# One fourth-layer product for two chunks, and a score tile ahead of the values, in a one-core vision layer

## The reference

```
h = concat(cls_tok, tok(x))
h = h + attention(layernorm(h))        # 16 heads of 16 features, causal
h = h + feed_forward(layernorm(h))

# attention, per head: queries and keys of low rank, RMS norm, q = [qn, W_QR qn], k = [kn, W_KR x]
out = softmax(q k^T / 4 + causal) v W_O^T

# feed forward
gf = sigmoid(gelu(gelu(mean_t(x) w1 + b1) w2 + b2) w3 + b3)          # global net: 256-128-64-1, one number per image
for _ in range(3):
    tf = sigmoid(gelu(gelu(gelu(out w1+b1) w2+b2) w3+b3) w4 + b4)    # coupling net: 256-256-128-64-1, one per token
    coupling = 0.1 + adaptive_range * (0.7 gf + 0.3 tf - 0.5) * 2
    out = out + coupling * twist(out)                                # twist swaps the halves, with signs
```

## Time and profile before

| | |
|---|---|
| median of three runs | 3649.94 us (3648.4 to 3652.1) |
| profiled execution | 3651.66 us, its span 3649.9 us |
| PE busy | 3549.6 us, 97% |
| PEld busy | 2676.6 us, 73% |
| DVE busy | 3088.9 us, 85% |
| ACT busy | 2422.8 us, 66% |
| POOL busy | 1827.4 us, 50% |
| mean granted PE clock | 0.989 of full speed |

### The profile page before, as it was taken

How to read it: one execution, slowest core, us unless ns; L and a number is a source line. 1 busy time by engine, 2 the same in 40 slices (tenths; PEclk the granted TensorE clock), 3 DMA queues, 4 the chain that set the end, 5 groups by cost and what they waited for, 6 DMA issues and landing times.

```text
span 3649.9 us, 88155 instructions
## 1 busy us (share of the span) xinstructions
PE 3549.6 (97%) x30735; PEld 2676.6 (73%) x30990; DVE 3088.9 (85%) x7415; ACT 2422.8 (66%) x5698; POOL 1827.4 (50%) x2967
## 2 busy tenths in 40 slices
PE   7999999999999999999999999987999999999998
PEld 6888888888888888888888888875555555555554
DVE  6888888888888888888888888876989989989987
ACT  4777777777777777777777777774554555554554
POOL 5776677666776667766777667763001001001000
PEclk9999999999999999999999999988999999999999
DMA  3444444444444444444444444433222222212211
GB/s 102 119 120 106 117 115 120 114 111 116 117 120 112 114 113 120 116 111 114 117 120 115 113 117 115 120 88 81 65 65 78 71 58 81 75 55 80 73 45 54
DMA packets 298324, 361.76 MB, mean 99 GB/s; under 512 B 28192, under 2 KB 264992, under 8 KB 297888
## 3 DMA queue, kind: packets, MB, share of 16 engines
q1 hardware_dynamic: 297888, 356.11, 37.2%
HBM read 131.80 MB, written 53.26 MB: 51 GB/s over the span
## 4 chain that ended last, share of the span: by engine, by line
PE 86%; DVE 7%; DMA 2%; issue 2%; SPq 1%; ACT 0%; POOL 0%; DVEq 0%; another core or an unknown queue 0%; POOLq 0%
PE ps L1077 14%; PE ps L1411 11%; PE ps L1165 8%; PE ps L1126 7%; PE ps L1113 7%; PE ps L1420 6%; PE ps L1196 5%; PE ps L1150 5%; PE ps L1215 4%; PE ps L1205 3%; PE ps L1173 3%; PE ps L1435 2%; PE ps L1427 2%; PE ps L1154 2%; PE ps L1198 2%
## 5 line engine op out<-in xcount | busy, mean ns | idle before, releaser
L1077 PE MATMUL ps<-xb,w_tok 128*128 128x196 f32 x3072 | 686.3, 348 | 7.5 <-DMA clsT<-in_clsT 7.3
L1411 PE MATMUL ps<-X,cn_w 128*128 128x394 f32 x1536 | 584.9, 510 | 7.7 <-DVE X L1015 7.7
L886 DVE TENSOR_REDUCE mx<-ps 69x2 f32<-69x396 f32 x1024 | 518.0, 553 | 14.2 <-PE ps L1205 1.3
L592 ACT ACTIVATE p<-ps 128x394 f32<-128x394 f32 x1024 | 454.8, 499 | 74.6 <-PE ps L1126 65.3
L1077 PEld LDWEIGHTS ps<-xb,w_tok 128*128 128x128 f32 x3072 | 491.7, 192 | 8.0 <-DMA clsT<-in_clsT 7.3
L880 DVE TENSOR_REDUCE mx<-ps 128x4 f32<-128x512 f32 x512 | 337.6, 680 | 181.1 <-remote 180.2
L543 POOL TENSOR_SCALAR ve<-mv 128x4 f32<-128x4 f32 x64 | 20.2, 316 | 911.7 <-DVE mv L898 911.7
L1411 PEld LDWEIGHTS ps<-X,cn_w 128*128 128x128 f32 x1536 | 273.6, 189 | 258.0 <-issue 94.9
L537 POOL TENSOR_TENSOR h<-h,att 128x256 f32<-128x256 f32 (+1 forms) x256 | 186.9, 751 | 431.9 <-DVE att L875 431.9
L1126 PE MATMUL ps<-qZ,kT 128*128 128x396 f32 (+1 forms) x2048 | 382.5, 320 | 12.9 <-DMA qZ<-mx_scratch 11.0
L610 ACT ACTIVATE sq<-ps 128x256 f32<-128x256 f32 (+1 forms) x512 | 196.2, 383 | 247.1 <-PE ps L1113 247.1
(11 more groups left out here) (139 smaller groups left out, 8076.5 us busy)
## 6 DMA issues: line engine op xcount, KB each, us to landing
qZ<-qT SPq DMA_DIRECT2D x256, 396.0 KB, 5.2
xb<-in_x SPq DMA_DIRECT2D x128, 588.0 KB, 7.2
kZ<-kT SPq DMA_DIRECT2D x512, 128.0 KB, 2.6
h_scratch<-h SPq DMA_DIRECT2D x128, 128.0 KB
hl<-h_scratch SPq DMA_DIRECT2D x64, 256.0 KB
hk<-h_scratch SPq DMA_DIRECT2D x64, 256.0 KB
out<-hk SPq DMA_DIRECT2D x64, 256.0 KB
h_scratch<-h SPq DMA_DIRECT2D x128, 69.0 KB
```

Of the source, the lines that this page charges most:

```text
L592: s.activation(p0[:, i, 2 * jj:2 * jj + 2, :], ps[:, (b0, b1)[jj], 0:2 * TE].rearrange("p (a b) -> p a b", b=TE)[:, :, 0:T], ACT.Exp).then ...
L886: v.tensor_reduce(mx[:T1, 1, 4 * i + c:4 * i + 4:2], ps[:T1, SBANK[3 * i + 1 + c], 0:2 * TE].rearrange("p (a b) -> p a b", b=TE), AX.X, AL ...
L1077: mm = t_.matmul(ps[:, W[ft], 0:NP], w_tok[:, k, ft * P:ft * P + P], xb[:, par, k, :], start=k == 0, stop=k == KT - 1)
L1411: mm = t_.matmul(ps[:, 2 * c + mt, 0:N2], cn_w1[:, f, mt * P:mt * P + P], X[:, c, state(cyc), f, :], start=f == 0, stop=f == FT - 1)
```

## The change

Four things are changed.

1. Layer 4 is one product of 128 rows. `cn_w4r` is now block diagonal: the weights stand in rows 0 to 63 for columns 0 to 63 and in rows 64 to 127 for columns 64 to 127, and zeros elsewhere. So output partitions 0 to 63 hold the first chunk's result, 64 to 127 the second's, in one bank. As `th` must hold each chunk's result in all 128 partitions, ACT now runs two tanh passes of 64 partitions for each chunk: four passes per turn in place of two.
2. The last product of the global net is padded to 128 rows with zeros (`gc_w3r`, `ga2`).
3. DVE clears and fills these tiles once, ahead of the second stage: six operations in place of two, and one more wait.
4. The first tile of group 2 (`scores_first(m, 2)`, with its waits) stands ahead of the values of image o. Banks 0 and 1 change their roles in several tables, so that this tile's bank is freed by the second reduction (`MAX_OF` 2) instead of the fourth.

```
-        SBANK = (6, 7, 0, 1, 2, 3, 0, 1, 2, 3, 0, 5)
-        MAX_OF = (4, 2, 5, 6, 7)
+        SBANK = (6, 7, 0, 1, 2, 3, 1, 0, 2, 3, 1, 5)
+        MAX_OF = (2, 4, 5, 6, 7)
...
             def tanh(i, cyc, c):
-                act.wait_ge(l4_done[c // 2], (i * CYCLES + cyc) * 2 + c % 2 + 1)
-                s.activation(th[:, c, :], ps[:, 4 * (c // 2) + 3 * (c % 2), 0:N2], ACT.Tanh, bias=cn_b4[:, 1:2],
-                             scale=0.5).then_inc(th_ready[c], 1)
+                G, e = divmod(c, 2)
+                rows = slice(e * F3, e * F3 + F3)
+                act.wait_ge(l4_done[G], i * CYCLES + cyc + 1)
+                for to in (slice(0, F3), slice(F3, 2 * F3)):
+                    s.activation(th[to, c, :], ps[rows, 4 * G + 3, 0:N2], ACT.Tanh, bias=cn_b4[rows, 1:2],
+                                 scale=0.5).then_inc(th_ready[c], 1)
...
-            v.tensor_copy(cn_w4r[:], cn_w4[:, 0:1].to_broadcast([2 * F3, P])).then_inc(s_ff, 1)
-            v.tensor_copy(gc_w3r[:], gc_w3[:, 0:1].to_broadcast([G2, P])).then_inc(s_ff, 1)
+            v.memset(cn_w4r[:], 0.0).then_inc(s_ff, 1)
+            v.memset(gc_w3r[G2:P, :], 0.0).then_inc(s_ff, 1)
+            v.memset(ga2[G2:P], 0.0).then_inc(s_ff, 1)
+            v.tensor_copy(gc_w3r[:G2, :], gc_w3[:, 0:1].to_broadcast([G2, P])).then_inc(s_ff, 1)
+            dve.wait_ge(s_ff, 4)
+            for e in range(2):
+                rows = slice(e * F3, e * F3 + F3)
+                v.tensor_copy(cn_w4r[rows, rows], cn_w4[rows, 0:1].to_broadcast([F3, F3])).then_inc(s_ff, 1)
...
+                if there(m):
+                    pe.wait_ge(kZ_loaded[1], n * 32)
+                    scores_first(m, 2)
                 if there(o):
                     if there(m):
                         pe.wait_ge(s_max, n * 12 - 11)
...
-                    scores_first(m, 2)
                     scores_halves(m, 1 - r % 2, 2)
...
             def layer4(i, cyc, G):
                 pe.wait_ge(a3_ready[G], i * CYCLES + cyc + 1)
-                for e in range(2):
-                    rows = slice(e * F3, e * F3 + F3)
-                    t_.matmul(ps[:, 4 * G + 3 * e, 0:N2], cn_w4r[rows, :], a3[rows, G, :], start=True, stop=True)\
-                      .then_inc(l4_done[G], 1)
+                t_.matmul(ps[:, 4 * G + 3, 0:N2], cn_w4r[:], a3[:, G, :], start=True, stop=True).then_inc(l4_done[G], 1)
```

More of the change, by code:

```diff
@@ L105, in build @@
         gc_w3 = sb("gc_w3", [G2, 1])
-        gc_w3r = sb("gc_w3r", [G2, P])
+        gc_w3r = sb("gc_w3r", [P, P])
+        ga2 = sb("ga2", [P, 2, 4])
         gc_b1 = sb("gc_b1", [G1, 1])
@@ L160, in build @@
         ga1 = sb("ga1", [G1, 2, 4])
-        ga2 = sb("ga2", [G2, 2, 4])
         gth = sb("gth", [P, 2, 4])
@@ L179, in build @@
         SETS = ((0, 1, 2), (3, 4, 5))
-        SBANK = (6, 7, 0, 1, 2, 3, 0, 1, 2, 3, 0, 5)
-        MAX_OF = (4, 2, 5, 6, 7)
+        SBANK = (6, 7, 0, 1, 2, 3, 1, 0, 2, 3, 1, 5)
+        MAX_OF = (2, 4, 5, 6, 7)
         W = (6, 7)
-        KB, QB = (3, 4, 0, 5), (1, 2, 3, 4)
+        KB, QB = (3, 4, 1, 5), (0, 2, 3, 4)
         HB = (4, 5)
         PB = ((4, 6), (4, 7))
-        MB, CB = (7, 0), (1, 2)
+        MB, CB = (7, 1), (0, 2)
         s_w = sem("weights_loaded")
@@ L700, in gnet @@
                 elif l == 1:
-                    s.activation(ga2[:, G, :], ps[:G2, b2, 0:4], ACT.Gelu, bias=gc_b2[:, 0:1])\
+                    s.activation(ga2[:G2, G, :], ps[:G2, b2, 0:4], ACT.Gelu, bias=gc_b2[:, 0:1])\
                      .then_inc(g_ready[G], 1)
@@ L972, in _ @@
             v.tensor_scalar(c_base[:], sign[:], 0.1, None, ALU.mult).then_inc(s_ff, 1)
-            dve.wait_ge(s_ff, 7)
+            dve.wait_ge(s_ff, 11)
             def gsums(i, c):
@@ L1007, in update @@
                 old, new = X[:, c, state(cyc)], X[:, c, state(cyc + 1)]
-                dve.wait_ge(th_ready[c], n)
+                dve.wait_ge(th_ready[c], 2 * n)
                 v.scalar_tensor_tensor(u0[:, e, :], old[:, 1, :], c_tf[:, 0:1], th[:, c, :], ALU.mult, ALU.mult)\
@@ L1485, in _ @@
                     for c in (2 * O, 2 * O + 1):
-                        pe.wait_ge(th_ready[c], oi * CYCLES + ocyc + 1)
+                        pe.wait_ge(th_ready[c], (oi * CYCLES + ocyc + 1) * 2)
                         x_transpose(oi + 1, c)
```

## The result

The changed kernel takes 3612.95 us (median, 3608.24 to 3614.95), the one before 3649.89 (3648.4 to 3652.1). The ratio is 0.9896, with a 95% interval of 0.9884 to 0.9908: 1.0% faster, and within a microsecond of the 3612 forecast. The profiled execution took 3614.95 us with a span of 3612.9, against 3651.66 before.

What follows compares the result with a forecast made beforehand. PE was taken to bound both stages; 20.0 us from the feed forward and 17.6 from the score tile, 37.6 off the 3649.9 median, gave 3612.3, rounded to 3612 us, range 3598 to 3634.

Steps and rivals of the forecast that it cites:

- PE sets both stages: Attention stage and feed forward: PE busy 2375.6 of 2420 and 1084.4 of 1100 us, so gains come from denser instructions.
- Layer 4, 0.40 a turn: Layer 4's product in neighbours' shape: two shape switches go, 0.41 summed, taken as 0.40 us a turn; halved count brings nothing.
- The three terms: Products ahead of layer 4 from 1.52 to 1.42 us, layer 4 from 0.87 to 0.66, products behind from 2.75 to 2.65.
- The tanh: ACT behind layer 4: four passes over 64 partitions at 0.48 us each; turn 5's update starts 1.97 behind layer 4.
- rival D: Slower: four tanh passes hold up PE; sign turns at 0.69 us apiece; 3726 us at 0.89 apiece; chance 0.04.
- Who feels it: Transposes back in turns 5 and 6 feel the 0.38 us later tanh, 0.28 lost; a quad gains 1.32.
- The feed forward, -20: 63 turns at 0.40 give 25.2 us, less 4.2 at 15 quad ends and about 0.9 at the end: -20 us.
- Global net and clears, 0: Global net's padding before the transposes and once-only DVE clears before the first turn's DMA wait: 0, clears at most 1 us.
- The tile, -17.6: Score tile ahead of the values in the attention stage: one shape switch less, 0.14 us in 126 images, -17.6 us.
- A: The tile waits: the hand-over in the attention stage eats the switch; 3630 us, chance 0.12.
- B: Tanh not felt in turns 5 and 6, PE gains everywhere, 47 us instead of 20; 3585 us, chance 0.05.
- C: DVE takes the feed forward: 3 us of new gaps on DVE leave PE no gain; 3632 us, chance 0.12.

Runs made afterwards that it cites:

- the kernel above: Changed kernel in which a chunk's second tanh pass reads and writes the same 64 partitions as its first, into an unused attention tile: 3609.29 us, ratio 0.9889.

## Why the prediction was right

**PE sets both stages, read from neighbouring starts: right.** Every saving showed as a shorter distance between starts.

**Layer 4, 0.40 a turn: right, and for the reason given.** The three terms came out at 0.10, 0.21 and 0.10. That the halved count brought nothing beyond the switches follows from the two padded products: four full-height passes take 1.32, so the half-height ones, at 0.87 with two switches of 0.10, had run in pairs. The Trainium skill's rule on products on distinct row groups (TensorE: Matmul & The Clock Gate, Part 3) holds in this case, with 0.87 us for four passes.

**The tanh: the mechanism right, one size off.** The step that failed is "so I take 0.48 again" for a pass over 64 partitions: it is 0.61. The prediction named its blind spot itself, that no row showed a pass "that writes other partitions than it reads"; with equal starts it is 0.49, as the kernel above shows, so the size was wrong by the move of the start, or by the crossing of partitions that goes with it within a chunk. From this one size the rest follows: update at 2.09 instead of 1.97, turn 5 at 13.44 instead of 13.30. ACT's four passes still held nothing else up: the next turns are 9.62, and PE waits for ACT nowhere new. At 0.61 a pass ACT stayed below the 0.69 at which rival D would have begun.

**Who feels it: right.** Turns 5 and 6 alone, the transposes back, with 13.63 us of DVE from one update to the next (13.61 taken). In turns 1 to 3 the update starts 2.79, 3.18 and 3.59 behind layer 4, before 2.69 in each: DVE falls back by 0.40 a turn, as computed, and nothing waits for it. From layer 4 of turn 5 to that of the next quad there are 26.54 us, where 26.39 were put. The loss per quad is 0.42, not 0.28, the gain 1.18, not 1.32. A quad can be split so: start of the update behind layer 4 in turn 5, DVE's time to its next update, what is left from there to the next quad, and turns 1 to 4. Before 1.59 + 13.61 + 10.91 + 43.44 = 69.55; after 2.09 + 13.63 + 10.81 + 41.84 = 68.37; with the transposes later 2.09 + 13.64 + 10.04 + 41.84 = 67.61. The split holds by itself; what the runs add is that DVE's time (13.62 to 13.63) and the 10.81 (2.57 + 8.24 in the prediction) came out the same in after and in all nine variants of it that leave the transposes in place. So where turns 1 to 4 are alike the first term alone decides: 1.55 goes with 67.82 (two tanh passes), 1.96 with 68.23 (equal starts).

**The feed forward, -20: -18.3** (18.8 less the 0.5 behind the last layer 4). At 15 quad ends 0.14 more is lost than was put, 2.1 us. The first turn of the first quad, which I gave nothing because it waits for DMAs, took 19.73 instead of 20.51; but it lies between 17.5 and 21.4 in the profiles of all versions, so these 0.8 say nothing. The last turn (11.77 instead of 11.27) and the tail lost 1.0, where 0.9 was put.

**Global net and clears, 0: right.** Shown by the kernel with 64 rows: no difference, with 9 us of work turned into wait.

**The tile, -17.6: -18.7 in the profile, and 7.7 to 17.9 in the run of this part alone.** Between the mean starts of the first layer 4 in the profiles of either order there are 18.4. The image's median fell by 0.16 (mean 0.15) where 0.14 was put, and the stretch from transposes to half tiles by 0.15. It fits by 0.03 us, as computed; that this margin is real is shown from the other side, by the tile 0.3 us earlier, which loses 0.30.

**The rivals.** A (the tile waits) did not happen, but it is what happens one step earlier or with the old banks. B is out by turn 5. C is out: DVE waits 0.31 us for the tanh in turn 4, so it had caught up. 0.19 was computed; with the measured 0.50 in place of 0.38 the same sum gives 0.31. Its condition was set too low, though: 3 us of new gaps on DVE make 42.1 + 3 = 45.1, still under PE's 45.5, and it would have taken 4.3 for PE to gain nothing. D did not reach its point.

So the time came out within 1 us partly by luck: the feed forward gained 1.7 less and the attention stage, in the profiled executions, 1.1 more than was put. And the time of one kernel differs by up to 7 us between its runs (3608.24 to 3614.95), so the terms are judged by the lengths of turns and images and not by the total.

## What to carry to other kernels

A small product of another shape costs what stands around it, not its passes: read the distances between starts from the neighbour ahead to the one behind, and give it the neighbours' shape if zeros can fill it. Before counting what a denser engine wins, close the loop: where two engines hand work back and forth, a result that comes later adds in full at the one place where it is awaited, and what is saved ahead of that place becomes waiting. When a slot for a moved tile is bound by a buffer, move the buffer's release with it; here the same order was 3.6% slower than before with the old banks, and 1.0% faster with the new.

## What the runs showed of the hardware

- A pass on ACT over 394 elements follows the one ahead by 0.49 us if it starts at the same partition, over 64 partitions as over 128, and by 0.60 to 0.61 if the start moves between partitions 0 and 64. 0.60 was measured with input and output moving together (the kernel with equal starts). 0.61 was also measured where only the output's start moved, but there one pass writes other partitions than it reads; a move of the input alone wasn't tried. The pass itself takes 0.57 to 0.59 in either case.
- A product's change of shape on PE costs 0.10 us on leaving and 0.10 in the next shape's first pass, at each of the places where 64-row products of 394 columns were removed or put back; beside the 17-column value products one change less gave 0.14 to 0.16 an image.
- Four 64-row passes, two and two side by side, take 0.87 us; two passes of 128 rows 0.66; four of 128 rows 1.32.
- From the end of the DVE reduction that a PE product waits for to the start of that product there are 0.15 us, in every image of the two kernels whose tile waits.
